# Attention scores in two float32r parts on the two row halves of TensorE, instead of three bfloat16 parts on all rows, and one more mask by products

## What is computed

```
q, k, v = split_heads(norm(x) @ wq + bq), split_heads(ctx @ wk + bk), split_heads(ctx @ wv + bv)
logits  = einsum('bhqd,bhkd->bhqk', q, k) / sqrt(16)
layer 0:  logits + (1 - mask) * -1e9;  softmax;  attn * group_prob
layer 1:  where(mask == 0, -1e9, logits);  softmax
layer 2:  where(mask_of_keys, logits, -inf);  softmax
layer 3:  softmax
x = x + (attn @ v joined over heads) @ wo + bo
```

## Time and profile before

| | us |
|---|---|
| median of three executions | 1506.51 |
| lowest and highest | 1498.33, 1510.62 |
| span of the profiled execution (no other time of it is given) | 1502.7 |
| projection of the context | 0 to 255 |
| first attention | 255 to 530 |
| second attention | 614 to 847 |
| third attention | 965 to 1148 and its last heads |
| fourth attention | 1260 to 1440 and its last heads |

### The profile page before, as it was taken

The page is one execution under the profiler, slowest core; times in us unless marked ns, Lnnn a source line. Parts: engine busy times, 40 slices in busy tenths (PEclk is TensorE's granted clock), DMA queues, the critical chain, the costliest instruction groups (busy, mean ns, idle before and its releaser), DMA issues. The chain is left out here.

```text
span 1502.7 us, 28955 instructions
## 1 busy us (share of the span) xinstructions
PE 1371.0 (91%) x10502; PEld 810.9 (54%) x10576; DVE 1010.4 (67%) x2314; ACT 857.6 (57%) x1308; POOL 567.3 (38%) x686
## 2 busy tenths in 40 slices
PE   8999797999999888699999888699999896999987
PEld 3766655455555456255555555255555582555555
DVE  4445486999999724778787053588884236888832
ACT  5143141899999621288888551167777211777762
POOL 4564252689989800655555340111110001111100
PEclk9999999799999978799999999899999998999999
DMA  8878998255456062266655195247776801667800
GB/s 265 280 255 256 245 258 274 33 77 83 65 82 146 2 89 39 53 96 90 88 81 143 59 185 202 75 71 109 104 113 190 118 9 45 96 96 108 156 2 8
DMA packets 126008, 178.30 MB, mean 119 GB/s; under 512 B 14733, under 2 KB 106021, under 8 KB 116646
## 3 DMA queue, kind: packets, MB, share of 16 engines
q1 hardware_dynamic: 111898, 161.04, 52.1%
q10 hardware_dynamic: 13968, 15.41, 3.4%
HBM read 132.58 MB, written 43.78 MB: 117 GB/s over the span
## 5 line engine op out<-in xcount | busy, mean ns | idle before, releaser
L1003 ACT ACTIVATE prob_a<-ps 128x1024 f32<-128x1024 f32 x464 | 456.6, 1020 | 142.7 <-PE ps L835 95.4
L818 PE MATMUL ps<-kop,qop 116*128 116x512 bf16 x1024 | 344.9, 401 | 37.4 <-DMA qop<-qparts 22.9
L1027 DVE TENSOR_REDUCE best_a<-ps 128x1 f32<-128x512 f32 (+1 forms) x488 | 318.5, 709 | 48.9 <-PE ps L818 48.4
L835 PE MATMUL ps<-qop,kop 116*128 116x256 bf16 x2048 | 333.9, 274 | 7.1 <-ACT prob_a L1003 2.6
L835 PEld LDWEIGHTS ps<-qop,kop 116*128 116x128 bf16 x2048 | 193.8, 98 | 123.2 <-ACT prob_a L1003 20.7
L1023 DVE CUSTOM_DVE_ANT_0 dump_a<-ps,neg_q 128x512 bf16<-128x512 f32 (+1 forms) x244 | 165.7, 715 | 43.5 <-PE ps L818 41.3
L862 PE MATMUL ps<-prob_a,vop_a 128*32 128x256 f32 x3072 | 191.7, 383 | 3.1 <-POOL prob_a L1167 2.2
L818 PEld LDWEIGHTS ps<-kop,qop 116*128 116x128 bf16 x1024 | 95.3, 103 | 162.4 <-issue 65.5
L1137 POOL TENSOR_TENSOR used_a<-prob_a,gT 128x1024 f32<-128x1024 f32 x64 | 153.2, 2396 | 23.6 <-DVE used_a L1040 17.0
L1116 POOL CAST mpart_a<-nmax_a 128x2 bf16<-128x2 f32 x64 | 26.4, 412 | 351.9 <-DVE nmax_a L1032 351.9
L1167 POOL TENSOR_TENSOR prob_a<-prob_a,neg_k 128x1024 f32<-128x1024 f32 x48 | 102.5, 2135 | 92.0 <-ACT prob_a L1001 86.4
(11 more groups left out here) (337 smaller groups left out, 1823.1 us busy)
## 6 DMA issues: line engine op xcount, KB each, us to landing
kop<-kparts SPq DMA_DIRECT2D x448, 128.0 KB, 5.1
kparts<-kp SPq DMA_DIRECT2D x64, 384.0 KB, 4.5
vals<-vst SPq DMA_DIRECT2D x16, 1024.0 KB, 5.3
vraw<-vals SPq DMA_DIRECT2D x64, 256.0 KB, 6.6
e_w<-in_e_w SPq DMA_DIRECT2D x4, 2048.0 KB, 11.0
z_w<-in_z_w SPq DMA_DIRECT2D x24, 256.0 KB, 6.8
ctxT<-in_ctxT SPq DMA_DIRECT2D x8, 512.0 KB, 8.1
raw<-in_mask ACTq DMA_DIRECT2D x16, 256.0 KB, 5.5
```

The costliest lines, as they stand in the source:

```text
L818: return pe.matmul(out, qop[0:R_ALL, h, t * P:(t + 1) * P], kop[0:R_ALL, h % UNROLL, j * CHUNK:(j + 1) * CHUNK], start=True, stop=True)
L835: ins = pe.matmul(st_bank(n)[:, j * NT:(j + 1) * NT], kop[0:R_ALL, h % UNROLL, k * P:(k + 1) * P], qop[0:R_ALL, h, :], start=(j % 2 == 0), ...
L1003: act.activation(prob[:, n % NP, :], st_bank(n), ACT.Exp).then_inc(S("exp_done"), 1)
L1027: dve.tensor_reduce(out, bank, AX.X, ALU.max).then_inc(sem, 1)
```

## The change

Keys, queries and the row maximum are split into two parts of type float32r instead of three of bfloat16. A score's operand has 51 rows: 16 of high key with high query, 16 of high key with low query, two for the maximum, one for the mask of keys, 16 of low key with high query. `kop` holds 2048 keys on rows 0 to 50 and the other 2048 on rows 64 to 114; `qop` has the queries on both halves. Chunks alternate between the halves but for two places (`chunk_keys`), the four products of a group alternate within it and write two banks, and the mask's two products follow all four. Key tiles are permuted to suit (`key_tile`), in the layout of the inputs too. The split of keys has two steps (ACT, VectorE) instead of four, and 512 KB are stored per unit instead of 384; a head's keys come in six pieces of 128 KB instead of seven. The maximum is split in two steps, turned by float32r products, and placed by two instructions of ACT. `SHIELD` is empty: in layer 1 TensorE masks all eight groups. All of `qop` is cleared beforehand, its first four heads by VectorE, the rest by GpSimd; SyncE waits for that before it loads the rest of the queries.

```diff
-PARTS_BESIDE = [3, 2, 2]
-PAIRS = [(k, q) for k, n in enumerate(PARTS_BESIDE) for q in range(n)]
-R_MAX = 96
-R_MASK = R_MAX + 3
...
+HALVES = 2
+HROWS = P // HALVES
+HKEYS = KEYS // HALVES
+R_MAX = 2 * HD
+R_MASK = R_MAX + 2
+R_LOW = R_MASK + 1
+R_ALL = R_LOW + HD
+HIGH, LOW = 0, 1
+K_PIECES = [(half, part, half * HROWS + row) for part, row in ((HIGH, 0), (HIGH, HD), (LOW, R_LOW)) for half in range(HALVES)]
...
+GROUP_AT = [0, 2, 1, 3, 4, 6, 5, 7]
+half_rows = lambda half: slice(half * HROWS, half * HROWS + R_ALL)
+
+def key_tile(i):
+
+    g, j = i // GROUP, i % GROUP
+    return HKEYS // P * (j // 2) + 2 * GROUP_AT.index(g) + j % 2
+
+def chunk_keys(j):
+
+    n = NCHUNK // HALVES
+    return (j + j // n) % HALVES, j % n * CHUNK
...
-        self.kop = ctx.enter_context(c.nc.sbuf_tensor("kop", [P, UNROLL, KEYS], BF16))
+        self.kop = ctx.enter_context(c.nc.sbuf_tensor("kop", [P, UNROLL, HKEYS], F32R))
...
-            def second(u):
-                act.wait_ge(S("k_rest"), u + 1)
-                act.activation(kp[:, u % SLOTS, 1, :], rest[:, u % RESTS, :], ACT.Copy).then_inc(S("k_second"), 1)
...
-                    dve.wait_ge(S("k_first"), u + 1)
-                    if u >= RESTS:
-                        dve.wait_ge(S("k_split"), u - RESTS + 1)
-                    dve.scalar_tensor_tensor(out=rest[:, u % RESTS, :], in0=c.ps[:, K_BANKS[u % 4], :],
...
+                    dve.wait_ge(S("k_high"), u + 1)
+                    dve.scalar_tensor_tensor(out=kp[:, u % SLOTS, LOW, :], in0=c.ps[:, K_BANKS[u % 4], :],
...
-            def third(u):
-                pool.wait_ge(S("k_second"), u + 1)
-                pool.tensor_tensor(kp[:, u % SLOTS, 2, :], rest[:, u % RESTS, :], kp[:, u % SLOTS, 1, :], ALU.subtract)\
-                    .then_inc(S("k_split"), 1)
+            pool.memset(c.qop[:, UNROLL:H, :].bitcast(F32), 0.0).then_inc(S("qop_rest_set"), 1)
...
-    SHIELD = (2, 5, 7) if l == SHIELDED else ()
+    SHIELD = ()
...
-            return pe.matmul(out, qop[0:R_ALL, h, t * P:(t + 1) * P],
-                             kop[0:R_ALL, h % UNROLL, j * CHUNK:(j + 1) * CHUNK], start=True, stop=True)
+            half, first = chunk_keys(j)
+            rows = half_rows(half)
+            return pe.matmul(out, qop[rows, h, t * P:(t + 1) * P], kop[rows, h % UNROLL, first:first + CHUNK],
+                             start=True, stop=True)
...
-            for j in range(GROUP):
-                k = g * GROUP + j
+            for j in (0, 2, 1, 3):
+                half, at = divmod(key_tile(g * GROUP + j) * P, HKEYS)
+                rows = half_rows(half)
                 added = by_query and g not in SHIELD and g not in own
...
+                ins = pe.matmul(st_bank(n)[:, j * NT:(j + 1) * NT], kop[rows, h % UNROLL, at:at + P], qop[rows, h, :],
+                                start=(j % 2 == 0), stop=(not added and j % 2 == 1))
+            if added:
+                for j in (0, 2):
+                    k = g * GROUP + j
+                    ins = pe.matmul(st_bank(n)[:, j * NT:(j + 2) * NT], c.identb[:, :], c.neg_k[:, k:k + 2, :],
+                                    start=False, stop=True)
...
-                ins = pe.matmul(turn_out[0:R_MASK, t * P:(t + 1) * P], mpart[:, h % 2, t, :], c.identb[:, :],
+                ins = pe.matmul(turn_out[:, t * P:(t + 1) * P], mpart[:, h % 2, t, :], c.identr[:, :],
...
-            act.activation(qop[R_MAX:R_MASK, h, :], turn_out[R_MAX:R_MASK, :], ACT.Copy).then_inc(S("max_set"), 1)
+            for half in range(HALVES):
+                rows = slice(half * HROWS + R_MAX, half * HROWS + R_MASK)
+                act.activation(qop[rows, h, :], turn_out[rows, :], ACT.Copy).then_inc(S("max_set"), 1)
...
-        c.kparts = nc.dram_tensor("kparts", (LAYERS, 3, D, KEYS), BF16).ap()
-        c.qparts = nc.dram_tensor("qparts", (3 * HD, H, NT), BF16).ap()
+        c.kparts = nc.dram_tensor("kparts", (LAYERS, PARTS, D, KEYS), F32).ap()
+        c.qparts = nc.dram_tensor("qparts", (PARTS * HD, H, NT), F32).ap()
```

More of the change, by code:

```diff
@@ L17 @@
 BF16 = mybir.dt.bfloat16
+F32R = mybir.dt.float32r
 I32 = mybir.dt.int32
@@ L262, in load @@
     def load(self, eng, l, h):
-        for piece in range(len(PAIRS) + 1):
+        for piece in range(len(K_PIECES) + 1):
             self.load_piece(eng, l, h, piece)
@@ L273, in load_q, with __init__ @@
         for rows, at in pieces:
-            eng.dma_start(self.c.qop[at:at + rows.stop - rows.start, heads, :], self.c.qparts[rows, heads, :])\
+            eng.dma_start(self.c.qop[at:at + rows.stop - rows.start, heads, :].bitcast(F32), self.c.qparts[rows, heads, :])\
                .then_inc(sem, 16)
 class QueryParts:
-    def __init__(self, c, l, rest, qp):
-        self.c, self.l, self.rest, self.qp = c, l, rest, qp
+    def __init__(self, c, l, qp):
+        self.c, self.l, self.qp = c, l, qp
     def half(self, tile, mt):
@@ L301, in first_and_second, with low @@
             act.wait_ge(S("q_psum"), mt + 1)
-            act.activation(self.half(self.qp[:, 0, :], mt), c.ps[:, banks[mt], 0:NT], ACT.Identity,
+            act.activation(self.half(self.qp[:, HIGH, :], mt), c.ps[:, banks[mt], 0:NT], ACT.Identity,
                            bias=c.bq[:, self.l, mt:mt + 1]).then_inc(S("q_part0"), 1)
[L304 to L308, removed]
+    def low(self, dve, S, banks):
         c = self.c
@@ L348, in project_context @@
     FIND_AT = 5
-    SLOTS, RESTS = 5, 2
+    SLOTS = 5
     EARLY = 4
@@ L681, in _ @@
         norm_dve(c, dve, S, c.x, c.xn)
-        dve.memset(c.qop[96:P, :, :], 0.0).then_inc(S("qop_set"), 1)
-        q.rest_and_third(dve, S, banks)
+        dve.memset(c.qop[:, 0:UNROLL, :].bitcast(F32), 0.0).then_inc(S("qop_set"), 1)
+        q.low(dve, S, banks)
         if l == SHIELDED:
@@ L1107, in _ @@
     def _(pool):
-        step = Chain(pool, S("max_step"))
         def split(h):
@@ L2699, in lay_out @@
     out["ctxT"] = np.ascontiguousarray(i["ctx_1024"][0].T)
-    out["gT"] = np.ascontiguousarray(i["fside_BxSxS2_0"][0].T)
-    out["mask"] = i["mask_BxSxS2_ik1"][0]
-    out["maskT"] = np.ascontiguousarray(i["mask_BxSxS2_ik1"][0].T)
+    chunk_at = [half * HKEYS + at for half, at in map(chunk_keys, range(NCHUNK))]
+    by_chunk = np.concatenate([np.arange(at, at + CHUNK) for at in chunk_at])
+    by_tile = np.concatenate([np.arange(P * key_tile(k), P * key_tile(k) + P) for k in range(KT)])
+    out["gT"] = np.ascontiguousarray(i["fside_BxSxS2_0"][0].T[by_tile])
+    out["mask"] = np.ascontiguousarray(i["mask_BxSxS2_ik1"][0][:, by_chunk])
+    out["maskT"] = np.ascontiguousarray(i["mask_BxSxS2_ik1"][0].T[by_tile])
     out["mask_keys"] = np.ascontiguousarray(i["mask_Bx1xS2_bf1"][0]).view(np.uint8)
```

151 lines of the change are left out of this document (74 added, 77 removed).

## The result

The changed kernel takes 1568.11 us (median of 4 runs, 1560.23 to 1577.94) against 1506.11 before: 1.042 times as long, 95% interval 1.036 to 1.047. The forecast was 1510 us, within 1% of before, with a range up to 1540; the time lies outside it. The profiled execution took 1566.85 us with a span of 1565.6, 62.9 longer than before.

What follows compares the result with a forecast made beforehand. TensorE was taken to bound the second to fourth attentions, VectorE the first. Second attention +16, third and fourth -9, first +1, projection -4, queries -1 sum to +3: 1506.5 + 3 = 1510 us, range 1484 to 1540.

Steps and rivals of the forecast that it cites:

- two cycles: Rival, all attentions: a float32r column costs two cycles, so pairs only win back the loss; some 1700 us, chance 0.10.
- free switches: Rival, second attention: switching between masks and halves costs nothing, 12.0 us per head, -23 instead of +16; 1471 us, chance 0.06.
- the closing gap of VectorE: Rival, third and fourth attention: VectorE's waits vanish, 10.4 us per head, -36 instead of -9; 1483 us, chance 0.11.
- the -4: Projection, 0 to 255 us: fewer splitting steps against larger key stores; 4 us less, bounds -10 and +14.
- The second attention's sum: TensorE's time per head there, from scores, masks, values, switches, entries and turn: 14.7 against 13.6 us, +16 us in all.
- 0.02 for an entry: Second attention: cost in us per entry into row halves if float32r gets the fast weight load; +6 instead of +16 us.
- the turn's 0.14: Turning the maximum: two products of 128 columns with four-byte weights take 0.14 us more per head.
- I take 0.08: Bare weight load in us assumed per entry into row halves; 11 entries per head of the second attention, 0.9 us.
- moves the chunk forward by 0.22 at most: Third and fourth attention: the chunk VectorE waits for comes up to 0.22 us earlier per head, within a 0.3 gain.
- gives 0.08 back on re-entry: Third and fourth attention: returning to row halves costs 0.08 us per head, leaving a gain of 0.3, -9 us in all.
- beside the projection of the queries: GpSimd's memset of 12 heads was placed alongside that projection; queries, three times, -1 us in all (-3 to +2).
- Stores by the byte: Rival, projection: key stores cost by bytes, 1.72 us a unit instead of 1.29; +14 instead of -4, 1528 us, chance 0.13.

Runs made afterwards that it cites:

- the run with bf16: Changed kernel with bf16 in place of float32r everywhere, also in stores and loads of keys and queries: 1497.13 us, ratio 0.993 to the kernel before.
- the run with filled first heads: Changed kernel with bf16 whole-array filler products behind query products, in the attentions' first phase and where the first head lacks value products: 1577.12 us, ratio 1.046.
- the fastest version: Changed kernel with bf16 parts, GpSimd's clearing after VectorE's normalising, and groups 2, 5, 7 of the second attention masked by ACT and GpSimd: 1471.88 us, ratio 0.979.
- the run with the later weighting products: The fastest version plus fillers in the first heads, with VectorE's four weighting products per first-attention head one chunk later: 1494.5 us, ratio 0.993.
- the run with the wait: Changed kernel with GpSimd's clearing of the other 12 heads' query rows waiting until VectorE has normalised x: 1554.5 us, ratio 1.032.

## Why the prediction was wrong

**Right.** One cycle per float32r column (0.11 per 256), halves side by side, 0.09 to 0.10 for each switch, so three rivals fall: two cycles, free switches, and the closing gap of VectorE. The projection's -6.8 is near the -4, but no run takes its terms apart. The second attention's sum was sound to about 0.3 in all but one term: with 0.02 for an entry, and without the turn's 0.14 for a four-byte load, it makes 13.9, and the run with bf16, where the bare loads are gone, has 14.23.

**The entry into the half mode was mis-sized.** The step "I take 0.08" gave 0.9 per head. It is 0.11 to 0.12, the upper bound, and it isn't paid at entries alone: a single chunk that has waited for its bank starts with a bare load too, so the step from there into the values is 0.43 without any entry ahead of it. All bare loads together are 15.45 - 14.23 = 1.2 per head, where the prediction's entries and turn make 0.9 + 0.14 - 0.2 = 0.8 more than with bf16. That is 0.4 of the 0.75 by which the head is longer than the 14.7 forecast; the rest is the 0.3 of the other terms. The prediction had weighed the Trainium skill, "TensorE: Matmul & The Clock Gate", Fast Weight Load, which speaks of types other than FP32. By its load of 192 ns float32r belongs with FP32.

**In the third and fourth attention the sign failed.** The step that a faster TensorE "moves the chunk forward by 0.22 at most" and "gives 0.08 back on re-entry" mis-sized what is given back. The 0.22 came nearly in full: VectorE's first read of the four from 1078.98 lasts 0.69 and ends at 1079.67, and the chunk that waits for this bank starts at 1079.73, 0.06 behind, where it was 0.27 before (1046.0 and 1046.27). But the bare load then takes 0.12 on the way into the values (0.43 for 0.31) and 0.10 more behind them, from the next chunk to its read (1082.02 to 1082.55, before 1048.44 to 1048.87). So 0.22 is given back instead of 0.08, this gap stays at 1.09, and the new idle of 0.22 comes on top. Instead of -0.3 per head it is +0.28, of which the idles make 0.14; the rest was not taken apart. With bf16 the chunk comes as early, the two ways are 0.32 and 0.43, the gap is 0.87, and the head has -0.52.

**The clock was not priced.** The prediction looked at stretches where it was 1.00 and took the first heads to be like the others. The second intervals are 5.1, 2.9 and 2.9 us longer than the new periods, and the interval ahead of them in the second attention has grown by 2.2: some 13 us. That the low clock makes them long is shown by the run with filled first heads. With float32r the clock is unsteady in later heads too: of seven profiled executions with float32r in row halves five have heads of 13.6, of four with bf16 none. With bf16 the steady heads keep 1.00, while the third and fourth attention still start slowly (13.24 and 13.51), and in the fastest version the second as well. Why is open: no run separates the type from the row halves and from the order of work, and the same code gives different clocks (the second attention's second interval is 17.25 in the fastest version and 14.62 in the run with the later weighting products, which leaves that attention as it was).

**The memset "beside the projection of the queries" was misplaced.** It lies ahead of it, beside the normalising, and holds up VectorE: +14.5 instead of -1, and a wait of one line takes 13 of it back. The prediction named what hides GpSimd's time, and did not ask what VectorE does then. It did not price the clock of the query products either.

**The first attention** is bounded by VectorE as forecast, but its work grew: its weighting products take 1525 ns on average in seven heads from 334 us on, against 1422 before, four per head. That is the 0.4 by which its period grew. The last section shows what lengthens them.

**Stores by the byte.** That rival may have had the right mechanism with the wrong price. No +14 appeared: the projection got shorter, with two copies per key unit fewer, though ScalarE's wait for stores grew from 17.4 to 29.2 us. But with bf16, where stores and loads of keys have half the bytes, it is 14 us shorter again.

## What to carry to other kernels

Price a change of TensorE's array mode as columns, switch and the bare weight load behind it, and take the load of the type that is really used; small groups of products between switches can lose more by it than they save in columns. Before work is moved off engines with time to spare onto the busiest one, price it as its plain columns there. When an instruction is put on a free GpSimd, look at what VectorE does at that moment.

## What the runs showed of the hardware

VectorE and GpSimd took turns to the hundredth of a microsecond. VectorE's weighting product and GpSimd's product in the first attention of the changed kernel:

```profile
415.55 1.64 DVE L1045 SCALAR_TENSOR_TENSOR used_a<-prob_a,gT 128x1024 f32<-128x1024 f32 x1
...
413.73 2.38 POOL L1141 TENSOR_TENSOR used_a<-prob_a,gT 128x1024 f32<-128x1024 f32 x1 [1.22 <-ACT prob_a L1008]
416.06 1.19 POOL L1120 CAST mpart_a<-nmax_a 128x4 fp32r<-128x4 f32 x1
```

GpSimd's product ends at 416.11, 0.56 behind VectorE's start, and 1.64 - 0.56 = 1.08; sixteen products in a row from 334 us on give 1.08 or 1.09 in this way (one that meets no GpSimd instruction takes 1.22). GpSimd's cast of four columns in turn lasts 1.19, and 0.19 in the third attention, and ends just behind VectorE's product. The Trainium skill, "SBUF — State Buffer", Who interferes with whom, says that the two engines share a pair of ports as an exclusive lock, which some kinds of VectorE's instructions need and which the earlier one holds for its whole instruction. These rows agree, and so does the memset ahead of the queries. There VectorE got its turn only behind three of GpSimd's instructions in a row. And not every instruction takes part: in the run with the wait, VectorE's own memset starts at 1291.81, beside the 2.66 us of GpSimd's from 1291.71, and lasts 0.91 as it does in the changed kernel.

A granted clock of 0.50 beside a TensorE that the trace calls busy for all of 11 us was not expected either: its busy time alone doesn't tell which level it gets.
